# The ends of three attentions: which engine makes the gate, when ScalarE makes it, and what reads the output projection

## The chip, the cores and the metric

The kernel runs on one core of one Trainium2 chip. The metric is the device time of one execution in microseconds. TensorE multiplies, VectorE (DVE) and ScalarE (ACT) work on SBUF and PSUM, GpSimd (POOL) on SBUF, and SyncE (SP) issues most DMAs. The engines run their own instruction streams and meet by semaphores.

## The reference

Four layers on x of shape 8 x 512 x 128 (batches, tokens, width). Each is `x = x + s * g`, with s from an attention-like part and g from a feed-forward part passed through silu, both fed by the same normalised x:

```
xn = _layernorm(x, axis=-1)
s = _L0_attn_ref(xn, ...)             # 16 heads of 8, no mask, no output projection
g = _silu(_L0_ffn_ref(xn, ...))       # ternary weights, 128 -> 512 -> 512 -> 512 -> 128
x = x + s * g
xn = _layernorm(x, axis=-1)
s = _L1_attn_ref(xn, Wq, Wk, Wv, Wo)  # causal; returns out @ Wo.T
g = _silu(_L1_ffn_ref(xn, ...))       # weights and activations quantised to 4 bits
x = x + s * g
xn = _layernorm(x, axis=-1)
s = _L2_attn_ref(xn, ...)             # causal, on an RMS norm of xn; returns xn2 + out @ Wo.T + bo
g = _silu(_L2_ffn_ref(xn, ...))       # two layers of local attention and a GLU
x = x + s * g
...                                   # layer 3: a recurrent memory and a mixture of experts
```

## The kernel before

A hardware loop runs over the 8 batches; one turn of it holds layers 0 to 2 of a batch and the projections and experts of layer 3. The memory of layer 3 runs for all batches after the loop. Inside a turn the work is cut into blocks. At the end of a block all engines meet, VectorE clears the semaphores, they meet again, and the next block starts.

The function `attention` is such a block and runs three times in a turn. It writes, for each engine, one instruction stream over steps s = 0 to 49. `at_step(s)` says what a step holds: row maxima of the scores (`first`, VectorE), the second scores and their exponentials (`second`, two a step from step 12 to 43, ScalarE, tile `probs` or `early`), the weighted sums of a group of heads (`weigh`, TensorE, bank 5), and `back`: ScalarE copies the sums to `oT`, TensorE turns them, and VectorE divides them into `att` (`rden`, then four multiplications). For the last group of heads `weigh` is at step 45 and `back` at step 47.

Other work of the turn is threaded between those steps by a `beside` object. It has one generator for each engine; `yield n` means that what follows is issued once the attention has come to step n, and `beside.run(...)` after the steps issues all that is left.

- First attention (layer 0): not causal, no output projection, beside it `TernaryFfn`. VectorE writes `K.g` from PSUM bank 6 at step 40; ScalarE turns it into silu(g) after the steps. TensorE ends with 12 filler matmuls on bank 3 (`keep_busy`).
- Second attention (layer 1): causal, with projection `w1_o`. Beside it `Fp4ThenExperts`, whose last ScalarE work (step `1 << 19`) is `K.g` = silu of bank 7. TensorE turns `att` (bank 0), ScalarE copies it to `oT`, TensorE projects (bank 1), then 8 fillers.
- Third attention (layer 2): causal, with projection `w2_ao` and bias `b2_ao`, `combine=False`. Beside it `GluThenQkv`. The same end without a gate; 8 fillers.

`Chain.do` issues a VectorE instruction and waits for it before the next one.

Of the kernel before, what the change touches and what calls it, by code (L numbers as in the profile page):

```python
# [11 lines left out]
ALU = mybir.AluOpType  # L12
ACT = mybir.ActivationFunctionType
AX = mybir.AxisListType

P = 128
BATCH, T, D = 8, 512, 128
NT = T // P
# [319 lines left out]
class Beside:  # L338
# [8 lines left out]
    FILLERS_FROM = 0  # L347

    FILLED = {}
    started = False  # L350

    def tensor(self, pe):
# [17 lines left out]
def attention(nc, K, causal, wo=None, bo=None, combine=True, beside=None, after_store=False,  # L370
# [19 lines left out]
    beside = beside or Beside()  # L390
# [3 lines left out]
    scale = float(1.0 / np.sqrt(HD))  # L394
# [22 lines left out]
    with ExitStack() as tmp:  # L417
# [5 lines left out]
        with nc.Block() as block:  # L423
# [98 lines left out]
            def _(act):  # L522
                for s in range(-beside.BEFORE, STEPS):
# [21 lines left out]
                                act.wait_ge(oturned, g - 1)  # L545
                            nc.scalar.activation(oT[:, g % 2, :], K.ps[:, 5, :], ACT.Identity).then_inc(oT_ready, 1)
                    beside.run(beside.on_scalar, s)
                beside.run(beside.on_scalar)
                if wo is not None:
                    act.wait_ge(att_turned, 1)  # L550
                    act.wait_ge(oturned, NG)
                    nc.scalar.activation(oT[:, 0, :], K.ps[:, 0, :], ACT.Identity).then_inc(attT_ready, 1)

            @block.sync
            def _(sp):
# [33 lines left out]
            def _(dve):  # L589
# [8 lines left out]
                for s in range(-beside.BEFORE, STEPS):  # L598
# [26 lines left out]
                        lower_parts(maxima)  # L625
                    beside.run(beside.on_vector, s)
                beside.run(beside.on_vector)
                if wo is not None:
                    dve.wait_ge(projected, 1)
                    o = K.ps[:, 1, :].rearrange("p (t d) -> p t d", t=NT)  # L630
                    ch.do(nc.vector.tensor_copy(K.att[:, :, :], o))
                if bo is not None:
                    ch.do(nc.vector.tensor_tensor(K.att[:, :, :], K.att[:, :, :],
                                                  bo[:, :].unsqueeze(1).to_broadcast([P, NT, D]), ALU.add))
                    nc.vector.tensor_tensor(K.att[:, :, :], K.att[:, :, :], K.xr[:, :, :], ALU.add)
                if combine:
                    dve.wait_ge(beside.g_ready, 1)
                    ch.do(nc.vector.tensor_tensor(K.att[:, :, :], K.att[:, :, :], K.g[:, :, :], ALU.mult))
                    nc.vector.tensor_tensor(K.x[:, :, :], (x_in or K.x)[:, :, :], K.att[:, :, :], ALU.add)
        K.clear(spread=True)  # L640

# [4 lines left out]
class TernaryFfn(Beside):  # L646
# [1 line left out]

    LAST_STEP = 12
    FILLED = {12: (5, 4)}  # L650
    OUT_STEP = 36

    def __init__(self, nc, K, ctx):
        self.nc, self.K = nc, K
        self.hid, self.gelu_done, self.out_done, self.g_in, self.g_ready = K.pool[24:29]
        self.h = K.region
        self.g = sbuf(nc, ctx, "hid_b", [P, 4, T])

    def tensor(self, pe):
        nc, K = self.nc, self.K  # L660
# [21 lines left out]
    def scalar(self, act):  # L682
        nc, K = self.nc, self.K
        for layer, (s, dst) in enumerate(((K.s0_h1, self.g), (K.s0_h2, self.h))):
            for c in range(4):
                n = 4 * layer + c
                yield (4 * n + 3) * self.LAST_STEP // 32
                act.wait_ge(self.hid, n + 1)
                nc.scalar.activation(dst[:, c, :], K.ps[:, 6 + n % 2, :], ACT.Gelu,
                                     scale=s[:, c:c + 1]).then_inc(self.gelu_done, 1)  # L690
        yield 1 << 19
        act.wait_ge(self.g_in, 1)
        nc.scalar.activation(K.g[:, :, :], K.g[:, :, :], ACT.Silu).then_inc(self.g_ready, 1)

    def vector(self, dve):
        nc, K = self.nc, self.K
        yield self.OUT_STEP + NT
        dve.wait_ge(self.out_done, 1)
        nc.vector.tensor_tensor(K.g[:, :, :], K.ps[:, 6, :].rearrange("p (t d) -> p t d", t=NT),
                                K.s0_3[:, :].unsqueeze(1).to_broadcast([P, NT, D]), ALU.mult).then_inc(self.g_in, 1)  # L700


class Fp4Ffn(Beside):
# [2372 lines left out]
```

## Time and profile before

| what | value |
|---|---|
| median of 3 runs | 4192.31 us (4190.34 to 4197.16) |
| the profiled execution's own time | 4196.52 us |
| its span from the first to the last instruction | 4193.1 us |
| busy share of PE, DVE, ACT, POOL | 84%, 60%, 43%, 20% |
| mean granted clock of TensorE | 0.939 |

The profile is that of one execution, taken by the hardware profiler. A busy TensorE is not TensorE at its peak: its matmuls are pipelined and their ends are modelled. A share of busy time is a mean over stages with different limits, so what a change at the end of a block does has to be read from the rows of that end. 4196.52 is 3.4 us more than the span; this lies around the program.

### The profile page before, as it was taken

The page shows a single profiled execution, that of the slowest core. Times are in us where ns is not written, and L with a number is a line of the kernel's source. Part 1 is how long each engine was busy: PE and PEld are TensorE (multiplying, and loading weights), DVE is VectorE, ACT ScalarE, POOL GpSimd, SP SyncE. Part 2 cuts the span into 40 slices and gives each one's busy share as a digit, 9 for nine tenths or more (in the row PEclk, how much of TensorE's full clock was granted, in tenths as well). Part 3 has the DMA queues.
Part 4 walks back from the last instruction along what each step waited for, and adds up shares of the span by engine and source line. Part 5 has one row for each costly group of instructions (what it writes and reads, how often), then busy time and mean ns, then how long its engine had stood idle before and what let it go on. Part 6 is the DMA issues. An engine that isn't in the chain of part 4 may idle for free. (4 is left out here: it accounts for less than half of the span.)

```text
span 4193.1 us, 55509 instructions
## 1 busy us (share of the span) xinstructions
PE 3506.4 (84%) x19466; PEld 1814.7 (43%) x19615; DVE 2530.1 (60%) x5500; ACT 1823.9 (43%) x3753; POOL 821.5 (20%) x721
## 2 busy tenths in 40 slices
PE   3988798888988889887988889888898879888867
PEld 1444444444344444454444443444434544444434
DVE  3566655666556655666556665566556665566655
ACT  1544444444443535444444444444354444444414
POOL 1023300331012400233003310124002230033114
PEclk9999999999999999999999999999999999999978
DMA  4000111001011010000111010110200001110130
GB/s 155 25 17 26 36 30 34 31 4 61 5 34 34 1 65 25 17 26 32 34 34 31 4 63 4 34 34 1 65 28 14 27 36 30 34 31 4 63 84 21
DMA packets 87847, 140.06 MB, mean 33 GB/s; under 512 B 12472, under 2 KB 62466, under 8 KB 85002
## 3 DMA queue, kind: packets, MB, share of 16 engines
q1 hardware_dynamic: 81042, 127.30, 9.5%
q10 hardware_dynamic: 6522, 9.06, 0.7%
q8 instruction: 169, 2.77, 0.3%
q14 instruction: 114, 0.93, 0.1%
HBM read 106.14 MB, written 29.39 MB: 32 GB/s over the span
## 5 line engine op out<-in xcount | busy, mean ns | idle before, releaser
L618 DVE TENSOR_REDUCE nmax<-banks 128x1 f32<-128x512 f32 (+3 forms) x1216 | 761.1, 658 | 392.5 <-PE banks L440 228.2
L538 ACT ACTIVATE probs<-banks 128x512 f32<-128x512 f32 (+3 forms) x1024 | 475.7, 526 | 302.9 <-PE banks L458 299.9
L440 PE MATMUL banks<-ks,qs 72*128 72x512 bf16 (+3 forms) x1536 | 464.1, 348 | 98.3 <-DVE nmax L618 68.3
L458 PE MATMUL banks<-qs,ks 74*128 74x512 bf16 (+3 forms) x1536 | 461.9, 338 | 41.2 <-ACT probs L538 17.2
L96 PE MATMUL banks<-filler,identb 128*128 128x512 bf16 x1576 | 427.9, 392 | 36.0 <-PEq L76 26.5
L440 PEld LDWEIGHTS banks<-ks,qs 72*128 72x128 bf16 x1536 | 144.0, 101 | 418.4 <-DVE nmax L618 246.2
L538 ACT ACTIVATE early<-banks 128x256 f32<-128x256 f32 (+3 forms) x512 | 198.1, 440 | 196.6 <-PE banks L458 196.6
L1295 ACT ACTIVATE probs<-banks,nm 128x192 f32<-128x192 f32 x512 | 172.6, 422 | 229.9 <-DVE nm L1247 229.9
L501 PE MATMUL banks<-probs,v 128*32 128x512 f32 (+3 forms) x2048 | 239.1, 539 | 32.4 <-POOL probs L584 22.9
L253 POOL TENSOR_TENSOR rstd<-var,neghalf 128x4 f32<-128x4 f32 (+1 forms) x16 | 21.2, 1324 | 1246.2 <-DVE var L204 1137.8
L96 PEld LDWEIGHTS banks<-filler,identb 128*128 128x128 bf16 x1712 | 171.5, 101 | 205.0 <-issue 63.5
L458 PEld LDWEIGHTS banks<-qs,ks 74*128 74x128 bf16 x1536 | 142.1, 100 | 234.6 <-ACT probs L538 79.0
L1329 POOL TENSOR_TENSOR probs<-probs,inv 128x768 f32<-128x768 f32 x128 | 187.1, 1467 | 259.7 <-DVE inv L1257 259.7
L603 DVE RECIPROCAL rden<-banks 128x16 f32<-128x16 f32 x96 | 24.4, 254 | 317.9 <-PE banks L474 317.0
L446 PE MATMUL banks<-mask_q,identb 128*128 128x128 bf16 (+2 forms) x704 | 186.2, 265 | 0.0
L1199 PE MATMUL banks<-ident,probs 128*128 128x128 f32 x896 | 141.5, 295 | 49.9 <-POOL probs L1329 32.5
L1254 DVE TENSOR_REDUCE total<-probs 128x4 f32<-128x768 f32 x128 | 122.0, 953 | 84.6 <-ACT probs L1295 80.4
L584 POOL TENSOR_SCALAR_AFFINE_SELECT probs<-probs 128x512 f32<-128x512 f32 x128 | 97.3, 760 | 382.4 <-ACT probs L538 382.4
L584 POOL TENSOR_SCALAR_AFFINE_SELECT early<-early 128x512 f32<-128x512 f32 x128 | 92.8, 725 | 397.8 <-ACT early L538 397.8
L1247 DVE TENSOR_REDUCE nm<-banks 128x4 f32<-128x768 f32 x128 | 119.9, 937 | 64.1 <-PE banks L1180 63.9
L1990 PE MATMUL banks<-xnT,w_up_s 128*128 128x512 f32 x320 | 150.6, 609 | 1.4
L1199 PEld LDWEIGHTS banks<-ident,probs 128*128 128x128 f32 x896 | 101.2, 147 | 89.6 <-POOL probs L1329 47.4
(453 smaller groups left out, 6528.2 us busy)
## 6 DMA issues: line engine op xcount, KB each, us to landing
qs<-parts_scratch SPq DMA_DIRECT2D x300, 96.0 KB
ks<-parts_scratch SPq DMA_DIRECT2D x288, 96.0 KB
parts_scratch<-parts SPq DMA_DIRECT2D x50, 384.0 KB, 2.5
shared<-in_w_h SPq DMA_DIRECT2D x17, 1024.0 KB, 7.6
shared<-in_w SPq DMA_DIRECT2D x25, 256.0 KB, 4.0
qs<-max_parts SPq DMA_DIRECT2D x192, 4.0 KB
xn<-in_x SPq DMA_DIRECT2D x9, 256.0 KB, 2.7
factor_scratch<-g SPq DMA_DIRECT2D x9, 256.0 KB, 2.2
```

The costliest lines, as they stand in the source:

```text
L96: nc.tensor.matmul(K.ps[:, bank, :], K.identb[:, :], K.filler[:, :], start=True, stop=True)
L440: mm = nc.tensor.matmul(K.ps[:, b, i * keys:(i + 1) * keys], K.qs[0:72, 4 * g + j, t * P:(t + 1) * P], K.ks[0:72, 4 * g + j, 0:keys], star ...
L446: mm = nc.tensor.matmul(diagonal, K.identb[:, :], K.mask_q[:, :].unsqueeze(1).to_broadcast([P, n_heads, P]), start=False, stop=True)
L458: nc.tensor.matmul(K.ps[:, b, q0:T], K.ks[0:KR, h, k * P:(k + 1) * P], K.qs[0:KR, h, q0:T], start=True, stop=True).then_inc(scored2, 1)
L501: mm = nc.tensor.matmul(K.ps[32 * j:32 * j + 32, 5, q0:T], K.v32[:, k, 4 * g + j, :], probs[:, 4 * (q % QUADS) + j, q0:T], start=(k == 0), ...
L538: nc.scalar.activation(probs[:, 4 * (q % QUADS) + m % 4, q0:T], K.ps[:, bank("second", m), q0:T], ACT.Exp, scale=scale).then_inc(exped, 1)
L584: nc.gpsimd.affine_select(diagonal, diagonal, [[0, 4], [1, P]], ALU.is_ge, 0.0, base=0, channel_multiplier=-1).then_inc(masked, 1)
L618: nc.vector.tensor_reduce(nmax[:, t, h:h + len(heads)], K.ps[:, n % 2, 0:len(heads) * keys].rearrange("p (j k) -> p j k", k=keys), AX.X, A ...
L1199: mm = nc.tensor.transpose(K.ps[:, 4 + e, o:o + P], probs[:, w % RING, e, i, (k - t + 1) * P:(k - t + 2) * P], K.ident[:, :])
L1295: a = nc.scalar.activation(probs[:, w % RING, e, i, 64:256], K.ps[:, 2 * u + e, 256 * i + 64:256 * i + 256], ACT.Exp, bias=nm[:, u, e, i:i ...
L1329: nc.gpsimd.tensor_tensor(x, x, inv[:, w % 2, :, :].rearrange("p e t -> p (e t)").unsqueeze(2).to_broadcast([P, 4, SPAN]), ALU.mult).then_ ...
L1990: mm = nc.tensor.matmul(K.ps[:, 2 * (n % 2) + m, :], K.w3_up[:, e, (2 * m + c) * P:(2 * m + c + 1) * P], K.xnT[:, :], start=True, stop=True)
```

## The change

Three things are altered, in each of the 8 turns.

1. In every attention with a projection, what is left of the `beside` work on ScalarE now comes behind the copy of the turned output (`oT` for the projection), where it came ahead of it. The class constant `TURNED_FIRST = 1 << 18` lets work that is due at lower steps still go first. This concerns the second attention, whose gate is due at `1 << 19`.
2. The copy of the projection from PSUM to `att` is gone in the second and the third attention. The product with the gate (second) and the sum with the bias (third) read PSUM bank 1 in its place.
3. The gate of the first attention is no longer a Silu on ScalarE after the steps. ScalarE writes exp(-g) at step 42 into the tile `hid_b`, which is free by then; VectorE adds 1, takes the reciprocal and multiplies by g, also placed at step 42.

```
@@ class Beside
+    TURNED_FIRST = 1 << 18
@@ attention, scalar
-                beside.run(beside.on_scalar)
+                beside.run(beside.on_scalar, beside.TURNED_FIRST)
                 if wo is not None:
                     act.wait_ge(att_turned, 1)
                     act.wait_ge(oturned, NG)
                     nc.scalar.activation(oT[:, 0, :], K.ps[:, 0, :], ACT.Identity).then_inc(attT_ready, 1)
+                beside.run(beside.on_scalar)
@@ attention, vector
+                o = K.att[:, :, :]
                 if wo is not None:
                     dve.wait_ge(projected, 1)
                     o = K.ps[:, 1, :].rearrange("p (t d) -> p t d", t=NT)
-                    ch.do(nc.vector.tensor_copy(K.att[:, :, :], o))
                 if bo is not None:
-                    ch.do(nc.vector.tensor_tensor(K.att[:, :, :], K.att[:, :, :],
-                                                  bo[:, :].unsqueeze(1).to_broadcast([P, NT, D]), ALU.add))
+                    ch.do(nc.vector.tensor_tensor(K.att[:, :, :], o, bo[:, :].unsqueeze(1).to_broadcast([P, NT, D]),
+                                                  ALU.add))
                     nc.vector.tensor_tensor(K.att[:, :, :], K.att[:, :, :], K.xr[:, :, :], ALU.add)
                 if combine:
                     dve.wait_ge(beside.g_ready, 1)
-                    ch.do(nc.vector.tensor_tensor(K.att[:, :, :], K.att[:, :, :], K.g[:, :, :], ALU.mult))
+                    ch.do(nc.vector.tensor_tensor(K.att[:, :, :], o, K.g[:, :, :], ALU.mult))
                     nc.vector.tensor_tensor(K.x[:, :, :], (x_in or K.x)[:, :, :], K.att[:, :, :], ALU.add)
@@ class TernaryFfn
-    OUT_STEP = 36
+    OUT_STEP, GATE_STEP = 36, 42
+        self.e = self.g[:, 0, :].rearrange("p (t d) -> p t d", t=NT)
@@ TernaryFfn.scalar
-        yield 1 << 19
+        yield self.GATE_STEP
         act.wait_ge(self.g_in, 1)
-        nc.scalar.activation(K.g[:, :, :], K.g[:, :, :], ACT.Silu).then_inc(self.g_ready, 1)
+        nc.scalar.activation(self.e, K.g[:, :, :], ACT.Exp, scale=-1.0).then_inc(self.e_ready, 1)
@@ TernaryFfn.vector
+        yield self.GATE_STEP
+        dve.wait_ge(self.e_ready, 1)
+        ch.do(nc.vector.tensor_scalar(self.e, self.e, 1.0, None, ALU.add))
+        ch.do(nc.vector.reciprocal(self.e, self.e))
+        dve.wait_ge(self.g_in, 1)
+        nc.vector.tensor_tensor(K.g[:, :, :], K.g[:, :, :], self.e, ALU.mult).then_inc(self.g_ready, 1)
```

On ScalarE, from the last exponentials of the first attention into the next block (`prepare` for layer 1), the rows stood like this before:

```order
L538 ACTIVATE probs<-banks 128x512 x12
L546 ACTIVATE oT<-banks 128x512
L693 ACT_TABLE_LOAD
L693 ACTIVATE g<-g 128x512
L423 UNCONDITIONAL_BRANCH
L296 UNCONDITIONAL_BRANCH
L305 ACTIVATE prep_xnT<-banks 128x512
L308 ACTIVATE parts<-banks 128x512 x2
```

and stand like this now:

```order
L539 ACTIVATE probs<-banks 128x512 x10
L696 ACTIVATE hid_b<-g 128x512
L539 ACTIVATE probs<-banks 128x512 x2
L547 ACTIVATE oT<-banks 128x512
L424 UNCONDITIONAL_BRANCH
L296 UNCONDITIONAL_BRANCH
L305 ACTIVATE prep_xnT<-banks 128x512
L308 ACTIVATE parts<-banks 128x512 x2
```

The exponential of the gate stands ahead of the last two exponentials of the attention, and the load of a function table is gone from this place; it now stands behind the two `parts` rows, ahead of the first Silu of the next block.

On VectorE at the end of the same attention the rows were

```order
L699 TENSOR_TENSOR g<-banks,s_3_s 128x512
L603 RECIPROCAL rden<-banks 128x16
L605 TENSOR_TENSOR att<-banks,rden 128x32 x4
L638 TENSOR_TENSOR att<-att,g 128x512
L639 TENSOR_TENSOR x<-xn,att 128x512
```

and are now

```order
L703 TENSOR_TENSOR g<-banks,s_3_s 128x512
L707 TENSOR_SCALAR hid_b<-hid_b 128x512
L708 RECIPROCAL hid_b<-hid_b 128x512
L710 TENSOR_TENSOR g<-g,hid_b 128x512
L605 RECIPROCAL rden<-banks 128x16
L607 TENSOR_TENSOR att<-banks,rden 128x32 x4
L640 TENSOR_TENSOR att<-att,g 128x512
L641 TENSOR_TENSOR x<-xn,att 128x512
```

Three instructions on 512 columns stand ahead of the division of the last group of heads.

On ScalarE at the end of the second attention the rows were

```order
L546 ACTIVATE oT<-banks 128x512
L780 ACT_TABLE_LOAD
L780 ACTIVATE g<-banks 128x512
L552 ACTIVATE oT<-banks 128x512
L423 UNCONDITIONAL_BRANCH
```

and are now

```order
L547 ACTIVATE oT<-banks 128x512
L553 ACTIVATE oT<-banks 128x512
L790 ACT_TABLE_LOAD
L790 ACTIVATE g<-banks 128x512
L424 UNCONDITIONAL_BRANCH
```

The table load and the gate stand behind the second copy to `oT`. On the streams of TensorE, GpSimd and SyncE no row is added, removed or moved.

## Rows read from the trace of the kernel before

**Rows 1.** The page: busy time of each engine over the span.

```profile
PE 3506.4 (84%) x19466; PEld 1814.7 (43%) x19615; DVE 2530.1 (60%) x5500; ACT 1823.9 (43%) x3753; POOL 821.5 (20%) x721
```

**Rows 2.** Windows, one turn each: length, busy by engine, granted clock, DMA.

```profile
176.13:659.66 483.53, 412.56 (x2289) 212.83 (x2306) 298.53 (x640) 218.91 (x443) 93.76 (x81) 0.96 0.09 29
659.66:1152.06 492.40, 422.79 (x2289) 217.78 (x2306) 298.54 (x640) 218.82 (x443) 93.41 (x81) 0.94 0.09 29
```

**Rows 3.** Timeline, end of the first attention, turn 1: start, length, engine, line, [idle before].

```profile
168.35 2.06 ACT L538 ACTIVATE probs<-banks 128x512 f32<-128x512 f32 x4 [0.39 <-PE banks L458]
...
170.47 1.06 PE L501 MATMUL banks<-probs,v 128*32 128x512 f32 x8
...
172.22 1.28 ACT L693 ACT_TABLE_LOAD   x1
...
172.95 0.26 DVE L603 RECIPROCAL rden<-banks 128x16 f32<-128x16 f32 x1 [6.54 <-PE banks L474]
172.96 2.54 PE L96 MATMUL banks<-filler,identb 128*128 128x512 bf16 x11
173.24 0.48 DVE L605 TENSOR_TENSOR att<-banks,rden 128x32 f32<-128x32 f32 x4
173.51 0.63 ACT L693 ACTIVATE g<-g 128x512 f32<-128x512 f32 x1
174.65 0.69 DVE L638 TENSOR_TENSOR att<-att,g 128x512 f32<-128x512 f32 x1 [0.92 <-ACT g L693]
175.37 0.69 DVE L639 TENSOR_TENSOR x<-xn,att 128x512 f32<-128x512 f32 x1
...
177.19 0.87 DVE L197 BATCH_NORM_STATS2 stats<-x 128x6 f32<-128x128 f32 x4 [1.12 <-PEq L76]
```

**Rows 4.** Groups of VectorE instructions by form: busy, mean ns | idle before.

```profile
L699 DVE TENSOR_TENSOR g<-banks,s_s 128x512 f32<-128x512 f32 x8 | 5.5, 691 | 19.5 <-PE banks L678 19.5
...
L118 DVE TENSOR_SCALAR fp_steps<-h1T 128x512 uint16<-128x512 uint16 x8 | 3.4, 428 | 0.3
L112 DVE RECIPROCAL fp_rscale<-fp_scale 128x32 f32<-128x32 f32 x8 | 2.8, 353 | 0.3
L120 DVE TENSOR_SCALAR fp_steps<-fp_steps 128x512 bf16<-128x512 bf16 x8 | 2.3, 293 | 0.3
L112 DVE RECIPROCAL fp_rscale<-fp_scale 128x72 f32<-128x72 f32 x1 | 0.6, 602 | 0.0
```

**Rows 5.** Timeline, ScalarE in the block behind the first attention, turn 1.

```profile
186.63 0.60 ACT L879 ACTIVATE early<-banks 128x512 f32<-128x512 f32 x1 [2.01 <-PE banks L850]
187.76 1.23 ACT L314 ACTIVATE parts<-rest 128x512 bf16<-128x512 f32 x2 [0.54 <-DVE rest L232]
188.89 0.58 ACT L879 ACTIVATE early<-banks 128x512 f32<-128x512 f32 x1
```

**Rows 6.** Timeline, end of the second attention, turn 2.

```profile
766.70 0.60 ACT L552 ACTIVATE oT<-banks 128x512 f32<-128x512 f32 x1 [0.46 <-PE banks L512]
...
768.34 1.89 PE L96 MATMUL banks<-filler,identb 128*128 128x512 bf16 x8
768.64 0.69 DVE L631 COPY att<-banks 128x512 f32<-128x512 f32 x1 [2.69 <-PE banks L516]
769.37 0.69 DVE L638 TENSOR_TENSOR att<-att,g 128x512 f32<-128x512 f32 x1
770.09 0.69 DVE L639 TENSOR_TENSOR x<-x,att 128x512 f32<-128x512 f32 x1
```

**Rows 7.** Timeline, end of the third attention, turn 2.

```profile
944.57 2.80 PE L96 MATMUL banks<-filler,identb 128*128 128x512 bf16 x7 [0.22 <-issue]
...
945.93 0.69 DVE L635 TENSOR_TENSOR att<-att,xr 128x512 f32<-128x512 f32 x1
```

**Rows 8.** Windows at the fillers of the second attention, turns 1 and 2.

```profile
284.66:288.07 3.41, 3.41 (x10) 1.09 (x9) 2.08 (x3) 0.00 (x0) 0.00 (x0) 0.50 0.00 0
768.30:771.70 3.40, 1.93 (x10) 0.72 (x9) 2.07 (x3) 0.00 (x0) 0.00 (x0) 1.00 0.00 0
```

More of the change, by code:

```diff
@@ L650 @@
     FILLED = {12: (5, 4)}
-    OUT_STEP = 36
+    OUT_STEP, GATE_STEP = 36, 42
     def __init__(self, nc, K, ctx):
         self.nc, self.K = nc, K
-        self.hid, self.gelu_done, self.out_done, self.g_in, self.g_ready = K.pool[24:29]
+        self.hid, self.gelu_done, self.out_done, self.g_in, self.g_ready, self.e_ready, self.vec = K.pool[24:31]
         self.h = K.region
         self.g = sbuf(nc, ctx, "hid_b", [P, 4, T])
+        self.e = self.g[:, 0, :].rearrange("p (t d) -> p t d", t=NT)
     def tensor(self, pe):
@@ L690, in scalar @@
                                      scale=s[:, c:c + 1]).then_inc(self.gelu_done, 1)
-        yield 1 << 19
+        yield self.GATE_STEP
         act.wait_ge(self.g_in, 1)
-        nc.scalar.activation(K.g[:, :, :], K.g[:, :, :], ACT.Silu).then_inc(self.g_ready, 1)
+        nc.scalar.activation(self.e, K.g[:, :, :], ACT.Exp, scale=-1.0).then_inc(self.e_ready, 1)
     def vector(self, dve):
         nc, K = self.nc, self.K
+        ch = Chain(dve, self.vec)
         yield self.OUT_STEP + NT
```

## The prediction

> **What bounds the kernel now.** I read the page first: TensorE is busy 84% of the span, VectorE 60%, ScalarE 43% [rows 1]. This says only that no single engine fills the time. The windows of single turns say more: VectorE and ScalarE do the same work in each (298.5 and 218.9 us), yet a turn lasts 483.53 or 492.40 us, and the longer one has a granted clock of 0.94 where the shorter has 0.96 [rows 2]. So how the stretches of lower clock fall is worth up to 8.9 us a turn, whatever the code.
>
> The change touches three block ends, and a block ends when its last engine does. So I read the timeline of each end and ask which engine is last and which follows. In the first attention, turn 1, VectorE ends at 175.37 + 0.69 = 176.06, TensorE's fillers at 172.96 + 2.54 = 175.50, and the next block starts at 177.19, 1.13 behind VectorE [rows 3]. In the second, turn 2, VectorE ends at 770.78 and TensorE's fillers at 770.23 [rows 6]. In the third, turn 2, TensorE's fillers end at 947.37 and VectorE at 946.62 [rows 7]. VectorE is last in two of the ends and TensorE in the third; the most that a shorter VectorE tail can give is 0.56, 0.55 and 0 us.
>
> **Third attention: copy gone.** One VectorE instruction of 0.69 with 0.03 behind it leaves the tail. VectorE would end at 945.90, but the fillers end at 947.37 as before [rows 7]. Value 0. The sum with the bias now reads PSUM; a two-operand instruction of this shape that reads a bank takes 0.691 us, like one from SBUF [rows 4, 3]. What hides the gain is the eight fillers; without them it would be 0.72 x 8 = 5.8 us, and that is the lower bound of this term.
>
> **Second attention: copy to `oT` first, then the gate, no copy of the output.** Before, the copy to `oT` began at 766.70, 0.46 us after ScalarE had gone idle, and it waited for TensorE's transposes [rows 6]. So the gate was not in its way, and moving it gives this copy nothing. What the move costs: the table load (1.28, [rows 3]) and the gate (0.60, like the copy of the same shape) now come behind 767.30, so g is ready at 767.30 + 1.28 + 0.60 + 0.03 = 769.21. Queued behind it on ScalarE is only the block's end. VectorE's product waits for it, where it began at 769.37; it begins at about 769.25, and VectorE ends 0.12 earlier, less perhaps 0.05 for one more wait. The copy of 0.72 us was hiding a table load that has only moved. I take -0.1. In turn 1 these fillers run in a stretch of granted clock 0.50, TensorE is busy for the whole 3.41 us and is last; in turn 2 they have 1.00 [rows 8]. So seven turns count: -0.7 us. Bounds: 0, and +0.4 a turn if the delay named below shows up here (+2.8).
>
> **First attention: the gate at step 42.** ScalarE first. The last four exponentials take 2.06 us together, so with some 0.6 for one their starts are (2.06 - 0.6)/3 = 0.49 apart [rows 3]. The exponential of the gate goes between the second and the third of them, at 168.35 + 0.97 = 169.32, and takes 0.63 like the Silu on the same operands [rows 3]. ScalarE instructions that read SBUF and follow one another start 1.13/2 = 0.57 apart at most [rows 5], so the last two exponentials come 0.5 to 0.57 later. The last weighted sum (170.47) waits for them, and with it the `oT` copy, the transposes, the fillers: TensorE ends at 176.0 to 176.1 and no longer at 175.50. This alone uses up the 0.56 us that the end could give: however fast VectorE is, the end as a whole gains nothing.
>
> VectorE next. It has been idle for 6.54 us before 172.95 [rows 3], and the new work is meant for this hole. It starts when exp(-g) is ready: 169.32 + 0.63 + 0.04 = 169.99.
> - The sum with 1, 128x512 fp32 in SBUF, one input: no row has it. Between 0.293 (the bf16 form) and 0.69 (two inputs); the nearest is the one-input form on 512 elements at 0.428 [rows 4]. I take 0.43. End 170.42.
> - The reciprocal on 512 columns: rows have 353 ns for 32 columns and 602 for 72, which is 6.23 ns a column; the division of 16 columns takes 0.26 us, which lies on the same line (602 - 56 x 6.23 = 253) [rows 3, 4]. So 602 + 440 x 6.23 = 3341 ns. With 0.03 ahead: end 173.79. Bounds: 0.69, the price of every other instruction of this width, and a fifth more than the line.
> - The product with g, 0.69: end 174.52.
>
> The division for the last heads stands behind these in VectorE's order, as the rows in the section on the change show. Its input would be there at 172.95 + 0.55 = 173.50; it has to wait until 174.5. Then `rden` 0.26, `att` 0.48, the two products 0.69 each, with 0.03 between them: 174.45 + 0.26 + 0.03 + 0.48 + 0.03 + 0.69 + 0.03 + 0.69 = 176.66 to 176.7. Before it was 176.06. The gate is ready long before, so the 0.92 us of waiting for ScalarE [rows 3] goes; in its place stand 1.0 us behind the reciprocal and 0.55 behind the exponential. +0.6 us a turn, eight turns: +4.9.
>
> The table load that is gone here comes back in the next block ahead of its first Silu. That instruction begins at 186.63 after 2.01 us in which ScalarE waited for TensorE [rows 5]; a load of 1.28 fits. 0. Without this cover it would be 1.28 a turn.
>
> **A rule weighed.** The rows show 6.23 ns a column for the reciprocal [rows 4]. The Trainium skill, page "VectorE: DVE Perf Modes", section "First, the fixed hardware budget", says that reciprocal is an iterative divide with a repeat count of 8, on an engine of 0.96 GHz; taken as eight cycles a column this would be an estimated 8.3 ns, a reciprocal of 4.4 us, and some 8.5 us more than my sum in all. No row of this length tells; the three short forms speak for about six.
>
> **Sum.** 4.9 - 0.7 + 0 = +4.2 us. The profiled execution took 4196.52 and would take 4200.7; it is 4.2 above the median of 4192.31, so I put the sum on the median: 4196.5.
>
> **Rivals.**
> - Slower by more than can be told: the chain on VectorE is longer still. Before, the product with the gate began 0.5 us after the Silu ended at 174.14, an unexplained delay [rows 3]. If it stays ahead of that product (0.45 x 8 = 3.6) and the sum with 1 costs 0.69 (2.1), the total is +9.9: 4202.2. Or the reciprocal costs a fifth or more over the line on a long row (0.67 x 8 = 5.4: 4201.9; by the page's rule in the section above, 4205). It decides from 0.53 us a turn over my sum. Against it: the line of the short forms is straight, and the delay was behind a wait for another engine that will not be there. Chance 0.15.
> - No change, the reciprocal being cheap: at 0.69 us the gate is done at 171.9, ahead of `rden`, and VectorE would end at 175.7; TensorE, at 176.05, is then last, and the end is as before: 4191.6. This is the nearest to "the gate hides in the hole". Against it stands the line of the rows. Chance 0.08.
> - Faster: the clock. The same fillers met 0.50 in turn 1 and 1.00 in turn 2 [rows 8], and turns differ by 8.9 us [rows 2]. Half a microsecond more in each turn moves all later work against the stretches of lower clock. If three of the seven long turns became short ones by half that difference, 13 us go: 4183. Chance 0.10. The same the other way (+8: 4204): 0.15. For both speaks only that turns differ at all; against a large effect that three runs lie within 6.8 us.
> - The modelled ends of TensorE are wrong and the fillers do not hold the third end: -5.8, hence 4190.7. Chance 0.05.
>
> **How the numbers follow.** The forecast has 0.47; with its bounds (the sum with 1 from -1.1 to +2.1, the second end to +2.8) and some spread of the clock it reaches from 4191 to 4202. A measurement of this kernel tells 0.2%, 8.4 us, from no change: below 4183.9 is faster, above 4200.7 slower. Slower: 0.12 of the long chain, 0.11 of the bad clock, 0.06 of the forecast's own upper end, 0.29. Faster: most of the good clock, 0.07. Same: 0.64. For 8 in 10 the range reaches down half-way into the good clock and up over the long chain: 4185 to 4206.
>
> **What the profile after would show.** Right: a reciprocal of about 3.3 us on `hid_b`, followed by the product, with `rden` of the last group starting 1 us after its transposes; the last exponentials 0.55 later; VectorE last by some 0.6 us over TensorE in the first end; in the second the product beginning within 0.1 us of the gate's end, 0.1 earlier than before; the third end unchanged; no wait at the first Silu of the next block. Wrong: a reciprocal under 2.4 us, TensorE last in the first end, or turns whose lengths change by more than 1 us where their ends do not.

## The result and the profile after

| | before | after |
|---|---|---|
| median | 4194.1 us (4190.34 to 4197.16, 8 runs) | 4206.98 us (4196.24 to 4217.64, 8 runs) |
| profiled execution | 4196.52 us | 4196.24 us |
| its span, mean granted clock | 4193.1 us, 0.939 | 4192.4 us, 0.941 |

The changed kernel is slower: its median is 12.9 us higher, and the ratio over all runs is 1.0034, with a 95% interval from 1.0021 to 1.0047 (this ratio, here and below, can differ from the quotient of two medians in the fourth place). The forecast was 4196.5 with a range up to 4206.0. The first thing to see is that the profile does not contain this loss: the profiled execution after happens to be the shortest of its eight runs and is as long as that of before. The eight runs lie 21 us apart, and the longer ones have the lower mean clock: 4196.24 us at 0.941, 4217.64 at 0.936. So the profile can say what the ends of the blocks do, which hardly differs from turn to turn, and it has to be read with care for the total.

The page of after. TensorE has the same number of instructions; VectorE has eight more and 24.5 us more busy time than in [rows 1].

```profile
PE 3504.9 (84%) x19466; PEld 1813.4 (43%) x19615; DVE 2554.6 (61%) x5508; ACT 1822.4 (43%) x3753; POOL 819.8 (20%) x721
```

The timeline of the first attention's end in turn 1, which answers to [rows 3].

```profile
164.06 1.09 ACT L539 ACTIVATE probs<-banks 128x512 f32<-128x512 f32 x2 [0.39 <-PE banks L459]
...
165.03 0.63 ACT L696 ACTIVATE hid_b<-g 128x512 f32<-128x512 f32 x1
...
165.56 1.08 ACT L539 ACTIVATE probs<-banks 128x512 f32<-128x512 f32 x2
165.70 0.43 DVE L707 TENSOR_SCALAR hid_b<-hid_b 128x512 f32<-128x512 f32 x1 [3.58 <-ACT hid_b L696]
166.16 3.35 DVE L708 RECIPROCAL hid_b<-hid_b 128x512 f32<-128x512 f32 x1
...
166.69 1.06 PE L502 MATMUL banks<-probs,v 128*32 128x512 f32 x8 [0.59 <-ACT probs L539]
...
169.18 2.54 PE L96 MATMUL banks<-filler,identb 128*128 128x512 bf16 x11
169.55 0.69 DVE L710 TENSOR_TENSOR g<-g,hid_b 128x512 f32<-128x512 f32 x1
170.16 0.25 DVE L605 RECIPROCAL rden<-banks 128x16 f32<-128x16 f32 x1
170.44 0.48 DVE L607 TENSOR_TENSOR att<-banks,rden 128x32 f32<-128x32 f32 x4
171.02 0.69 DVE L640 TENSOR_TENSOR att<-att,g 128x512 f32<-128x512 f32 x1
171.74 0.69 DVE L641 TENSOR_TENSOR x<-xn,att 128x512 f32<-128x512 f32 x1
...
173.56 1.24 PE L96 MATMUL banks<-filler,identb 128*128 128x512 bf16 x5 [1.84 <-PEq L76]
```

The chain on VectorE is now unbroken from 165.70 to 172.43; `rden` no longer waits for TensorE: it stands in line behind the reciprocal and the product with g. The wait of 0.92 us for the Silu is gone. Measured from the start of the last four exponentials to VectorE's end: in [rows 3] 168.35 to 176.06, 7.71 us; here 164.06 to 172.43, 8.37 us. That is +0.66. Up to the point where the engines meet it is 8.43 to 8.44 us in all eight turns, 7.77 to 7.81 before.

The end of the second attention in turn 2, which answers to [rows 6].

```profile
765.88 0.60 ACT L553 ACTIVATE oT<-banks 128x512 f32<-128x512 f32 x1 [2.37 <-PE banks L513]
766.49 1.28 ACT L790 ACT_TABLE_LOAD   x1
...
767.52 1.89 PE L96 MATMUL banks<-filler,identb 128*128 128x512 bf16 x8
767.79 0.60 ACT L790 ACTIVATE g<-banks 128x512 f32<-128x512 f32 x1
768.52 0.69 DVE L640 TENSOR_TENSOR att<-banks,g 128x512 f32<-128x512 f32 x1 [3.38 <-ACT g L790]
769.24 0.69 DVE L641 TENSOR_TENSOR x<-x,att 128x512 f32<-128x512 f32 x1
```

The product begins 0.13 us behind the end of the gate (768.39). From the copy to `oT` to VectorE's end it is 769.93 - 765.88 = 4.05 us, against 770.78 - 766.70 = 4.08 in [rows 6]. In three of the eight turns, where it was one before, a stretch of half rate (granted clock 0.50) falls on TensorE's fillers here; then the end, from that copy to the meeting of the engines, takes 5.27 us and not 4.12.

The table load in the block behind the first attention, turn 1, which answers to [rows 5].

```profile
181.00 1.28 ACT L889 ACT_TABLE_LOAD   x1
183.00 0.60 ACT L889 ACTIVATE early<-banks 128x512 f32<-128x512 f32 x1 [0.71 <-PE banks L860]
```

The load fits into the wait for TensorE, of which 0.71 us is left. It costs nothing.

The end of the third attention in turn 2, which answers to [rows 7].

```profile
943.57 0.69 DVE L635 TENSOR_TENSOR att<-banks,b_ao_s 128x512 f32<-128x512 f32 x1 [4.13 <-PE banks L517]
943.66 2.78 PE L96 MATMUL banks<-filler,identb 128*128 128x512 bf16 x7 [0.22 <-issue]
...
944.30 0.69 DVE L637 TENSOR_TENSOR att<-att,xr 128x512 f32<-128x512 f32 x1
```

VectorE ends at 944.99, TensorE's fillers at 946.44: 1.45 us apart where they were 0.75 apart [rows 7]. The copy is gone and nothing came of it in this turn. Turn 1 is the exception: there the half rate has ended at 450.96, ahead of the projection, and the stretch from the copy to `oT` to the meeting takes 3.59 us. With the copy of the output still in place the trace of the delay with 15 fillers (below) has one such turn, its fourth, and it takes 4.15. So the removed copy is worth 0.56 us where TensorE runs at full rate; in the other seven turns half rate reaches into this end and hides it.

Windows, one turn each, which answer to [rows 2].

```profile
172.50:657.46 484.96, 414.70 (x2289) 214.45 (x2306) 301.88 (x641) 218.69 (x443) 93.65 (x81) 0.96 0.09 29
657.46:1151.77 494.31, 424.71 (x2289) 218.67 (x2306) 301.64 (x641) 218.74 (x443) 93.30 (x81) 0.94 0.09 29
```

The long turn is now 494.31 where 492.40 was; ScalarE and GpSimd are busy in it for as long as before, VectorE for 3.1 us more.

### The profile page after: what moved, and what is told of

It is laid out like the page before. It is cut to its first block and busy times, and to the rows that moved or that the text cites. A ratio compares the mean times of both kernels' runs of the same rounds, so it can differ in the third digit from the quotient of the medians.

```text
span 4192.4 us, 55525 instructions
## 1 busy us (share of the span) xinstructions
PE 3504.9 (84%) x19466; PEld 1813.4 (43%) x19615; DVE 2554.6 (61%) x5508; ACT 1822.4 (43%) x3753; POOL 819.8 (20%) x721
## 5 line engine op out<-in xcount | busy, mean ns | idle before, releaser
L441 PEld LDWEIGHTS banks<-ks,qs 72*128 72x128 bf16 x1536 | 143.4, 100 | 415.7 <-DVE nmax L620 245.3
```

Of the source, the lines that this page charges most:

```text
L441: mm = nc.tensor.matmul(K.ps[:, b, i * keys:(i + 1) * keys], K.qs[0:72, 4 * g + j, t * P:(t + 1) * P], K.ks[0:72, 4 * g + j, 0:keys], star ...
```

## The experiments

The theory to test: the loss is the longer tail of the first attention (+5.3 us in eight turns, -0.3 in the second), and the rest is TensorE's clock, because a turn of another length meets the stretches of half rate (granted clock 0.50, 1.2 GHz in place of 2.4) at other places. The rival: some part of the change costs more than its row shows, and would cost it again wherever it is put. The kernel before ran beside each experiment: 4193.14 us median beside the first four, 4194.69 beside the next four, 4192.38 beside the last four (17 to 23 runs each). "The grid" in the texts put down before the runs stands for the places in time where the stretches of half rate fall.

**The gate alone, on the kernel before.** Part 3 of the change without parts 1 and 2.

```
-        yield 1 << 19
+        yield self.GATE_STEP                                  # 42
-        nc.scalar.activation(K.g[:, :, :], K.g[:, :, :], ACT.Silu).then_inc(self.g_ready, 1)
+        nc.scalar.activation(self.e, K.g[:, :, :], ACT.Exp, scale=-1.0).then_inc(self.e_ready, 1)
+        ch.do(nc.vector.tensor_scalar(self.e, self.e, 1.0, None, ALU.add))
+        ch.do(nc.vector.reciprocal(self.e, self.e))
+        nc.vector.tensor_tensor(K.g[:, :, :], K.g[:, :, :], self.e, ALU.mult).then_inc(self.g_ready, 1)
```

> The kernel before with the change's third part alone: the gate of the first attention by an exponential at step 42; the second and third attention are as before. Two theories share the tail of the first attention, which lasts 0.66 us longer in the profile of the changed kernel (8.44 us from the last four exponentials to the meeting of the engines, 7.78 before), 5.3 us in eight turns. Theory of the tail: the whole difference of the change (+12.9 us between the medians) comes from what the instructions at the ends cost, so this kernel, which has all of the costly part, is slower by about 13 us. Theory of the clock: the tails give +5, and the rest comes from where TensorE's stretches at half rate fall once a turn is longer; this kernel is slower by 5 from the tails and by something between -5 and +12 from the clock, its runs scatter over more than 10 us, and a run with a lower mean clock is a longer one.

Measured: 4219.08 us (4205.0 to 4222.31, 6 runs), ratio 1.0058 [1.0043, 1.0072]. The tail is the 8.44 us of the changed kernel to the hundredth, and yet this kernel is 26 us slower than before, twice the loss of the whole change and more than either theory had allowed (13; 5 with up to 12 from the clock). Windows of its first two turns, and of a short piece of each that begins 15.2 and 15.4 us behind the first attention:

```profile
174.45:668.64 494.19, 426.09 (x2306) 218.80 (x2306) 302.82 (x643) 218.70 (x443) 93.33 (x81) 0.94 0.09 29
668.64:1152.28 483.64, 413.54 (x2306) 212.79 (x2306) 302.80 (x643) 218.64 (x443) 93.61 (x81) 0.96 0.09 29
...
189.64:193.05 3.41, 3.41 (x8) 1.86 (x9) 0.00 (x0) 0.60 (x1) 0.00 (x0) 0.50 0.29 103
684.00:687.41 3.41, 3.41 (x12) 1.72 (x11) 0.00 (x0) 1.19 (x2) 0.00 (x0) 1.00 0.29 86
```

TensorE is busy throughout in both short windows, with the same code; at 0.50 it gets 8 matmuls done, at 1.00 12. Where such a stretch falls is decided anew in each turn, and the turns differ by 10.5 us. From its fourth turn on this kernel alternates between 488.7 and 494.3.

**The copies alone.** Parts 1 and 2, the gate of the first attention as before.

```
-                beside.run(beside.on_scalar)
+                beside.run(beside.on_scalar, beside.TURNED_FIRST)
-                    ch.do(nc.vector.tensor_copy(K.att[:, :, :], o))
```

> The kernel before with the first two parts alone: no copies of the output projections, and the second gate behind the copy to oT; the gate of the first attention is the old Silu. Both theories: the second end is shorter by 0.03 to 0.13 us and the third the same, so the median lies within 3 us of the kernel before by the tails. Theory of the clock adds that even so small a shift may move the stretches: up to 5 us either way.

Measured: 4197.45 us (4189.41 to 4202.19, 11 runs), ratio 1.0007 [0.9999, 1.0016]: not to be told from before. The second end, taken from its first copy to `oT` to the meeting, is 7.08 us in six of the eight turns, 0.04 shorter than before; the third is held by TensorE's fillers. Alone the parts give +26 and +4, together +13. The first of these has an interval of 18 to 30 us and the last of 9 to 20, so the two just touch; as the medians stand the parts do not add up, and the total is no sum of the costs of instructions.

**A delay and nothing else.** The kernel before, with one more VectorE instruction of 0.72 us behind the wait for the gate in the first attention. It computes nothing that is used.

```
                 if combine:
                     dve.wait_ge(beside.g_ready, 1)
+                    if wo is None:
+                        spare = beside.g[:, 0, :]
+                        for n in (512,):
+                            ch.do(nc.vector.tensor_tensor(spare[:, 0:n], spare[:, 0:n], spare[:, 0:n], ALU.max))
```

> The kernel before with one extra instruction in each turn: at the end of the first attention, between the wait for the gate and the product with it, VectorE runs one two-operand instruction on 512 columns of a tile that is free there (0.69 + 0.03 us). Nothing else is changed. It lengthens the first end by 0.72 us, 5.8 us in eight turns, nearly what the changed kernel's first end does (0.66), with none of its other edits. Theory of the tail: +5.8 us and runs that lie as near to one another as those of before (7 us). Theory of the clock: like the changed kernel, +8 to +18 us, with a scatter of 10 us or more.

Measured: 4240.23 us (4231.06 to 4247.03, 4 runs), ratio 1.0108 [1.0091, 1.0125]. Eight instructions of 0.72 us, 5.8 us in all, cost +47 us, with the gate as before; +5.8 by the tail and +8 to +18 by the clock had been expected. The timeline of its turn 2 at the end of the first attention and behind it, and a window there:

```profile
665.32 2.75 PE L96 MATMUL banks<-filler,identb 128*128 128x512 bf16 x12
...
668.68 0.69 DVE L643 TENSOR_TENSOR x<-xn,att 128x512 f32<-128x512 f32 x1
...
670.50 4.65 PE L96 MATMUL banks<-filler,identb 128*128 128x512 bf16 x13 [2.42 <-PEq L76]
...
671.05:674.47 3.42, 3.42 (x10) 1.22 (x8) 2.19 (x12) 0.00 (x0) 1.01 (x1) 0.50 0.02 5
```

TensorE's fillers end at 668.07, VectorE at 669.37, and TensorE comes to the next block after 2.42 us of idling. In all eight turns a stretch of half rate now begins 0.55 to 1.22 us behind the first filler of the next block; the kernel before has none there in any turn. The same 13 fillers of the next block take 4.65 us here. In the kernel before they are quicker:

```profile
660.72 2.97 PE L96 MATMUL banks<-filler,identb 128*128 128x512 bf16 x13 [1.70 <-PEq L76]
```

**A longer delay.** The same with five such instructions, 3.41 us in all.

```
+                        for n in (512, 512, 512, 512, 300):
```

> The same with five such instructions, four of 512 columns and one of 300: 4 x 0.727 + 0.505 = 3.41 us a turn, 27.3 us in eight turns. [...] Theory that any delay costs more than its length (0.66 us that cost 1.6): +27 times a factor over 1, some +40 us or more. Theory of the tail: +27 too, so this run separates the clock from it only together with the delay of 0.7 us.

Measured: 4259.44 us (4257.82 to 4264.73, 5 runs), ratio 1.0161 [1.0148, 1.0174]: +66, of which 8 x 3.42 = 27 are its own length. In seven of the eight turns the half rate at this place now lasts 6.8 us and begins ahead of the meeting. If the stretches had fallen as before, +27 within 3 us was expected, and some +40 or more if a delay costs a multiple of its length; it is more than either.

**The delay with TensorE kept busy.** The delay of 0.72 us, and 15 fillers for 12.

```
-                keep_busy(nc, K, 3, 8 if causal else 12)
+                keep_busy(nc, K, 3, 8 if causal else 15)
```

> The kernel before with the extra VectorE instruction of 0.72 us a turn, as in the run that gave +47 us, and 15 fillers for 12 at the ends of the first attentions, so that TensorE is idle before the next block about as long as in the kernel before (1.7 us, where the delay alone makes it 2.4). Nothing is faster by itself. Theory of the idle TensorE: the longer idle time gives a stretch at half rate at the head of the next block in each turn (seen 1.4 to 2.1 us behind the meeting in all 8 turns of that run, in none of before); with the fillers it is gone, and most of the +47 with it: +6 by the delay, and by the grid from -3 to +20. Rival, that a delay of VectorE itself is what costs (its work in the next block, the position on the grid alone): the fillers change nothing, and it stays at +40 to +50.

Measured: 4214.05 us (4208.74 to 4217.8, 5 runs), ratio 1.0045 [1.0032, 1.0058]. Timeline and window of turn 2 at the same place:

```profile
667.71 2.97 PE L96 MATMUL banks<-filler,identb 128*128 128x512 bf16 x13 [1.78 <-PEq L76]
...
668.25:671.67 3.42, 3.38 (x16) 1.43 (x13) 2.20 (x12) 0.00 (x0) 1.01 (x1) 1.00 0.02 5
```

The idle time is 1.78 us, the stretch of half rate is gone and 28 of the 47 us with it. So two effects are apart: an idle gap of TensorE of 2.42 us was followed by half rate, and 19 us stay without such a stretch, of which the tail is 8 x 0.73 = 5.8. This is within what the theory of the clock allowed (+3 to +26), and against the rival that the fillers change nothing.

**The changed kernel with its idle gap filled.** After has only 0.14 us more of idle time than before (1.84 against 1.70). 15 fillers for 12 in the changed kernel, the edit shown above.

> The changed kernel with 15 fillers for 12 at the end of the first attention. VectorE was last there by 0.72 us, and three fillers take 0.65, so the tail keeps its length, and TensorE is idle 0.65 less before the next block. If what the changed kernel loses over its tails comes from TensorE being idle at this place, it is faster by some 5 to 8 us than the changed kernel (in it the next block has no stretch at half rate at its very head, but in some turns one 15 us behind the meeting). If it comes only from where the grid stands against the turn, this kernel is like the changed one: 4207 within 6 us.

Measured: 4208.85 us (4191.47 to 4220.04, 12 runs), ratio 1.0028 [1.0013, 1.0043], like the changed kernel without it. The first effect plays no part in the change; its loss is of the second kind.

**The gate's chain earlier.** The changed kernel with TernaryFfn's output and exponential four steps earlier and VectorE's part of the gate three, so that the gate is done ahead of `rden`.

```
-    OUT_STEP, GATE_STEP = 36, 42
+    OUT_STEP, EXP_STEP, GATE_STEP = 32, 38, 39
...
-        yield self.GATE_STEP                                  # ScalarE
+        yield self.EXP_STEP
```

> The changed kernel with its gate moved forward: TensorE makes the output of the feed-forward at steps 32 to 35 (36 to 39 before), ScalarE the exponential at step 38, VectorE the sum, the reciprocal and the product behind the division of step 39. My account of the tail: the reciprocal and the exponential then lie in idle time (VectorE 6.5 us, ScalarE 2.0 us ahead of the last eight exponentials), VectorE goes straight from the last division to the two products, and the end waits for TensorE's fillers: the stretch from the last four exponentials to the meeting is 7.2 us (8.44 in the changed kernel, 7.78 before), -10 us against the changed kernel and -4.6 against the one before, by the tails. Theory of the clock: on top of this the turns still take 484 to 495 us by where they meet the grid, so the median is 4188.5 with up to 10 us either way, and the table of turns and stretches tells how much. Theory of the tail alone: 4188.5 within 3 us.

Measured: 4215.27 us (4206.28 to 4219.11, 6 runs), ratio 1.0049 [1.0037, 1.0061]. The tail of the first attention is 7.20 us, 1.24 shorter than after and 0.58 shorter than before, with TensorE last by 0.27. All that was wanted of the end was got, 4.6 us in eight turns, and the kernel is 21 us slower than before, where 4188.5 with up to 10 us either way had been expected. Its turns 4 to 7 are all alike:

```profile
1640.16:2131.69 491.53, 424.29 (x2306) 217.73 (x2306) 301.56 (x641) 218.66 (x443) 93.39 (x81) 0.94 0.09 29
2131.69:2623.19 491.50, 424.40 (x2306) 217.81 (x2306) 301.57 (x641) 218.69 (x443) 93.39 (x81) 0.94 0.09 29
```

**The same with 14 fillers for 12.** The last end of the series before, 0.44 us longer.

> The kernel with the gate moved forward (its tails were 7.20 us as forecast, 4.6 us shorter in sum than before, and it ran 20.6 us slower), with 14 fillers for 12 at the end of the first attention. TensorE is last in that end, so the tail is longer by 2 x 0.216 = 0.43 us in each turn, 3.5 us in all, and nothing is taken away. [...] Theory of the clock: the longer tail takes the turn off this multiple, the turns take different lengths again (484 to 495), and the kernel is faster by 5 to 15 us although it does more: 4200 to 4210. Theory of the tail, or of a fixed cost of the moved gate: slower by 3.5 us: 4219.

Measured: 4204.32 us (4176.47 to 4219.66, 12 runs), ratio 1.002 [0.9996, 1.0045]. Work was added and the median fell by 11 us. The twelve runs fall apart: five between 4176 and 4183 at mean clocks 0.943 to 0.946, two at 4203 and 4206 at 0.938 and 0.937, five between 4213 and 4220 at 0.933 and 0.934. It is one program throughout. The median is a matter of how many of the runs fall into which group. The profiled execution, 4181.31 us, is of the shortest group.

**Four doses.** The kernel before with the delay as above, each filled with more fillers: 0.36 us with 14, 1.71 with 20, 3.41 with 28 (0.72 with 15 stands above).

```
+                        for n in (161,):                   # with 14 fillers
+                        for n in (512, 512, 61):           # with 20
+                        for n in (512, 512, 512, 512, 300):  # with 28
```

> The kernel before with a delay of 0.36 us (one VectorE instruction on 161 columns) and 14 fillers for 12 at the end of the first attention. Tails: +0.36 x 8 = +2.9. The same with 0.72 and 15 fillers gave +19. Theory of a price per delay, in proportion: +10. Theory of the clock: no proportion; +2.9 by the tails and from -5 to +20 by the grid, with turns of 484 to 495 us, and the sum of half-rate time in the loop going with the time.

> [...] Tails +13.7. [...] Theory of proportion between the measured 0.72 (+19) and its length: +45.

> The kernel before with the delay of 3.41 us a turn (+27.3 by its length; +66 measured with TensorE idle meanwhile) and 28 fillers for 12, so that TensorE is idle as long as in the kernel before. [...] Theory of the clock in full: both ways in which a delay can act on the clock are shut, TensorE's idle time at the end and the place on the grid; so the stretches fall as before and it costs its length: +27 within 4 us, and the half-rate time of the loop is that of before (413 us) within 20. If it stays over +40, the delay costs in another way.

| delay a turn | its length in 8 turns | median over before | runs |
|---|---|---|---|
| 0.36 us | 2.9 | +25 | 4214.5 to 4220.02, 5 |
| 0.72 us | 5.8 | +19 | 4208.74 to 4217.8, 5 |
| 1.71 us | 13.7 | +14 (+19 with the longest run) | 4180.97 to 4239.85, 11, and one of 4248.34 |
| 3.41 us | 27.3 | +36 | 4219.34 to 4230.1, 5 |

The cost is not in proportion to the delay. For the delay of 1.71 us +8 to +33 had been expected by the clock and +45 by proportion. The smallest dose shows best what happens. Windows of the last block of a turn (layer 3, lines 1967 and on), for the smallest dose and then, behind the dots, for the kernel before, turns 1 and 2:

```profile
530.94:569.67 38.73, 36.12 (x145) 20.91 (x146) 20.85 (x65) 18.85 (x23) 0.00 (x0) 0.91 0.26 80
1022.44:1061.18 38.74, 36.12 (x145) 20.91 (x146) 20.85 (x65) 18.85 (x23) 0.00 (x0) 0.91 0.25 80
...
530.42:566.17 35.75, 33.13 (x145) 19.26 (x146) 20.85 (x65) 18.86 (x23) 0.00 (x0) 1.00 0.29 86
1018.21:1056.93 38.72, 36.10 (x145) 20.89 (x146) 20.84 (x65) 18.86 (x23) 0.00 (x0) 0.91 0.26 80
```

The block has two lengths, 35.75 us at a clock of 1.00 and 38.7 at 0.91, the latter when 6.8 us of half rate fall in it; VectorE and ScalarE take the same in both. TensorE is busy for 93% of it, so little hides the half rate. In its eight turns the smallest dose has the long form eight times, the dose of 0.72 us seven times, the early gate with 12 fillers eight times, before three times, after four times, the early gate with 14 fillers never (in the profiled execution of each). Five more of the long form are 5 x 2.95 = 15 us, the greater part of what the smallest dose loses in its profile (4214.7 - 4193.1 = 21.6). The mean clock does not tell this: it is 0.939 in both profiles, and the half rate of the eight turns sums up to 409 us against 413 before, though it had been expected to go with the time. What half rate costs depends on where it falls: 6.8 us of it make the last block 3.0 us longer, and the block behind the third attention 1.0 us (36.0 without, 37.0 in turn 1 of the changed kernel).

The largest dose was expected within 4 us of its length and lies 9 above it, and its half rate was expected within 20 us of 413 and is 386; both were missed. Its profiled execution, the shortest of the five, is only 22.8 us above the profiled one of before, so the 9 us stand in no trace.

**Fewer fillers in the other two ends.** The copies alone with 5 fillers for 8 in the second and third attention, so that TensorE lets them end sooner.

```
-                keep_busy(nc, K, 3, 8 if causal else 12)
+                keep_busy(nc, K, 3, 5 if causal else 12)
```

> The kernel with the first two parts alone (no copies; Silu as before), with 5 fillers for 8 at the ends of the second and third attention. In the third end TensorE is last by 0.8 to 1.4 us with the copy gone, and three fillers take 0.65 to 1.3 us there. Theory of the tail: the third end now gives what the copy's removal promised, 0.7 us a turn and more, -6 to -8 us; the second end does not change, since VectorE is last. Theory of the clock: fewer fillers leave TensorE idle longer before local attention and before the RMS norm, so new stretches at half rate may come at the heads of these blocks; 0 to +30 us.

Measured: 4195.85 us (4194.36 to 4202.43, 11 runs), ratio 1.0007 [0.9998, 1.0016]. The third end is shorter by 0.2 to 1.1 us in a turn than in the kernel before, and half rate in the eight turns grows from 412 us (the copies with 8 fillers) to 491. The gain was got and given back. Its second end repeats what the delay showed at the first: in six turns TensorE is idle for 2.29 us there, and in all six half rate begins 0.06 to 0.93 us behind its restart, where neither the kernel before nor the copies with 8 fillers have any.

## Why the prediction was wrong

**Right, the ends.** By the prediction's own steps, the term and what it measured:

| step | forecast | measured |
|---|---|---|
| last exponentials later | 0.5 to 0.57 | 0.53 (third exponential) |
| sum with 1 | 0.43 us | 0.43 |
| reciprocal, 512 columns | 3341 ns | 3.35 us |
| `rden` to VectorE's end | 2.2 us | 2.27 |
| first end, a turn | +0.6 | +0.66 |
| second end, a turn, no half rate on it | -0.1 | -0.04 |
| third end | 0 | 0 in seven turns |
| table load in the next block | 0 | 0 |

The shift of the exponentials: the third of the last four begins 165.56 - 164.06 = 1.50 us behind the first, where it began 0.97 behind it in [rows 3] by the prediction's working. The sum of the ends is 8 x 0.66 - 8 x 0.04 = +5.0 us, where +4.2 was forecast. The rival of a reciprocal much longer than the line falls, and so does the cheap one. The rate is (3350 - 602) / 440 = 6.2 ns a column. The trace before had one more form that the line left out, 88 columns in 680 ns, 22 ns below it; nothing hung on that. The delay of 0.5 us behind a gate, which was to cost up to 0.4 a turn at the second end, is 0.13 there. The Trainium skill, page "VectorE: DVE Perf Modes", section "First, the fixed hardware budget", with its repeat count of 8 had stood for an estimated 4.4 us; the trace does not agree with that reading.

**Wrong, the clock.** The step that failed is the price of the rival "the clock": it was put as something that may go either way by 8 to 13 us with a chance of 0.25 in all, and was left out of the sum. The runs show in its place that every one of the edits that moved the first end moved the pattern of half rate too, and cost about 12 us or more (the early gate with 14 fillers with an interval that touches no change), one that shortened this end among them. None of the twelve variants has a median below that of the kernel before; the two that leave the first end alone are nearest (+4.3 and +1.2), though they moved the pattern too. The rival's faster side was also misread: it speaks of seven long turns, and of the seven full turns of before five are long (488.7 to 492.5 us) and two short. The remainder, 12.9 - 5.0 = 8 us, is of this kind; the traces below bear it out block by block. What else speaks for it: the runs of the changed kernel differ by 21 us and their mean clock with them; the same gate on the kernel before costs 26 us with the same tail; the gate with a shorter tail costs 21; a delay of 0.36 us with the gate untouched costs 25. That last one has neither exponential, reciprocal nor another table load, so a loss of this size needs none of them.

The prediction had the signs of it in hand. It read that turns of equal work differ by 8.9 us [rows 2] and that the fillers met 0.50 in one turn and 1.00 in the next [rows 8], and it concluded from three runs within 6.8 us that a large effect was unlikely. But these three runs are those of one program; they tell nothing of how the pattern of another program falls. Its own sign of being wrong, turns that change by more than 1 us where their ends do not, is there: the third turn went from 491.55 to 488.71 us.

**No hidden cost.** The rival that some part of the change costs more than its row shows can be tested in the traces, by blocks with the same amount of half rate. The block with the first attention without half rate and with 3.4 us of it, before and, behind the dots, after:

```profile
2521.71:2615.36 93.65, 87.17 (x398) 33.30 (x400) 48.06 (x91) 48.29 (x84) 0.00 (x0) 1.00 0.01 1
2036.95:2132.34 95.39, 88.87 (x398) 33.89 (x400) 48.06 (x91) 48.29 (x84) 0.00 (x0) 0.98 0.01 1
...
2520.78:2615.09 94.31, 87.17 (x398) 33.29 (x400) 52.46 (x94) 46.88 (x83) 0.00 (x0) 1.00 0.01 1
2035.39:2131.41 96.02, 88.87 (x398) 33.79 (x400) 52.47 (x94) 46.87 (x83) 0.00 (x0) 0.98 0.01 1
```

It is 0.66 and 0.63 us longer, which is the end and nothing else. The other blocks without half rate are as long as before to 0.04 us, and the last block is 35.75 or 38.7 us in both kernels.

**In the profiled executions.** Sums over eight turns show the trade in one run: the block with the first attention +4.6 us, the block with the second +3.9, the third attention's block -8.3, the last block +3.0 (one more of the long form), the loop +2.1 in all, and what precedes it 3.6 us shorter. The gain in the third attention's block comes with 122.9 us of half rate in it for 143.4. No profile of a long run of the changed kernel itself was taken. The nearest is that of the changed kernel with 15 fillers: its first end is as long (8.44 us), and its profiled execution took 4209.98 us. There the eight turns are 13.5 us longer than before: the block with the first attention +5.4, the block with the second +6.2 with 143.4 us of half rate for 133.1, the last block +3.0 with 27.3 for 20.5, and the third attention's 0.0; the others -1.1. The gain of the third attention's block is not had, and what lies over the ends lies where half rate was added. That the long runs of the changed kernel itself are like this is argued from their mean clocks. How much half rate there is does not decide it: at a mean clock of 0.939 two of its runs took 4205.58 and 4206.8 us, and 24 runs of the kernel before 4194.8 in the mean.

**What stays open.** Which pattern a turn of a given length settles into was not foretold once, neither its sign nor its size. Whether the kernel before stands on a favourable pattern because earlier versions were chosen by their time can't be seen from these runs. The 9 us that the largest dose costs beyond its length are not placed.

## What to carry to other kernels

Read the ends of blocks instruction by instruction: that arithmetic held to a few hundredths of a microsecond where no half rate fell on the end, and it shows at once where a shorter tail on one engine is worthless because another ends last. But where TensorE is busy for most of a loop turn and equal turns differ in length, half a microsecond in the turn can move the total by 20 us through the clock alone, so the range has to be at least as wide as the difference between equal turns times a good part of the turns. Judge such an edit by many runs and beside a delay that computes nothing: if the delay costs as much, the loss is no proof against the edit's own instructions. And compare blocks with the same amount of half rate in both traces: what differs there is the edit.

## What the runs showed of the hardware

An idle gap of TensorE of 2.42 us at the meeting of two blocks was followed by half rate within 1.3 us of its restart in eight of eight turns, one of 2.29 us at another end within 1.0 us in six of six; gaps of 1.70, 1.78 and 1.84 us at the first of these places by none. One program can settle into different patterns from run to run: 4176 to 4220 us with the early gate and 14 fillers, 4181 to 4240 with the delay of 1.71 us, both with the mean clock falling as the time grows (0.945 to 0.933, 0.949 to 0.934). And the mean clock alone doesn't price it: at 0.939 both the kernel before (span 4193.1) and the smallest dose (4214.7) ran, 21.6 us apart, because the half rate lay in other blocks.
